# A new deal of expert slots and output tiles over the groups, and the values of a score chunk multiplied one group later than its scores

## The reference

```python
xn = _layernorm(x)
x = x + attention(xn, Wq, Wk, Wv, Wo, bo) + ffn(xn, gate_w, gate_b, w1, w2)
# attention: 16 heads of 64, rotary q and k, causal mask, softmax over 1024 keys, output matrix Wo
# ffn: each of 32 experts takes its 8 best tokens of a batch, weighted into one vector,
#      h = gelu([vec, 1] @ w1[e]); o = [h, 1] @ w2[e]; o is scattered back to the 8 tokens
```

## Time and profile before

| | us |
|---|---|
| median of 3 runs | 1545.79 (1543.32 to 1549.16) |
| the profiled execution, its time | 1545.64 |
| its span, first to last instruction | 1543.8 |
| PE busy in it | 1374.1 |
| POOL busy | 984.9 |
| DVE busy | 887.9 |
| ACT busy | 625.5 |

### The profile page before, as it was taken

One profiled execution on the slowest core, in us unless ns is written; L12 is line 12 of the kernel. 1 busy time (PEld: TensorE's weight loads), 2 busy tenths in 40 slices (PEclk: granted clock), 3 DMA queues, 4 the chain that ended last, 5 costly groups with the idle time before them and its releaser, 6 DMA issues.

```text
span 1543.8 us, 31034 instructions
## 1 busy us (share of the span) xinstructions
PE 1374.1 (89%) x11644; PEld 890.6 (58%) x11644; DVE 887.9 (58%) x1200; ACT 625.5 (41%) x919; POOL 984.9 (64%) x664
## 2 busy tenths in 40 slices
PE   3547889888988879999999999999999999999976
PEld 2334555454554546766666577666666776666646
DVE  7434555566464455567666655657666556656633
ACT  1213434334443433344444433544444435544431
POOL 1033655555554555688887865888887658888861
PEclk9778999898898999999999999999999999999999
DMA  5675665666556441212123322121232211222111
GB/s 202 255 241 189 237 203 198 213 213 214 198 200 226 159 139 56 82 65 70 57 83 111 94 70 67 59 90 57 70 101 94 93 59 61 81 72 70 43 46 55
DMA packets 112959, 188.85 MB, mean 122 GB/s; under 512 B 30064, under 2 KB 49936, under 8 KB 112432
## 3 DMA queue, kind: packets, MB, share of 16 engines
q1 hardware_dynamic: 85312, 115.39, 22.7%
q10 hardware_dynamic: 27456, 71.34, 13.6%
q0 software_dynamic: 48, 0.13, 0.0%
HBM read 130.58 MB, written 22.54 MB: 99 GB/s over the span
## 4 chain that ended last, share of the span: by engine, by line
PE 76%; DVE 6%; issue 5%; DMA 3%; ACT 3%; SPq 1%; POOL 1%; ACTq 0%; DVEq 0%; POOLq 0%
PE t_pO L1161 17%; PE t_pF L1136 13%; PE t_pA L1068 8%; PE t_pB L1068 6%; PE t_pF L1122 5%; PE t_pC L1210 3%; PE t_pB L1210 3%; PE t_pA L1092 3%; DVE t_OT L928 3%; PE t_pC L1170 2%; PE t_pC L1092 2%; PE t_pA L1073 2%; PE t_pB L1195 2%; PE t_pB L1073 2%; PE t_pB L1185 1%
## 5 line engine op out<-in xcount | busy, mean ns | idle before, releaser
L779 POOL TENSOR_TENSOR t_acc<-t_acc,t_PT 128x1024 f32<-128x1024 f32 (+3 forms) x256 | 444.4, 1736 | 203.4 <-ACT t_PT L814 183.7
L756 POOL TENSOR_TENSOR t_swap<-t_swap,s_sin 128x512 f32<-128x512 f32 x128 | 168.3, 1315 | 212.5 <-DMA t_swap<-t_raw 211.9
L1161 PE MATMUL t_pO<-t_PT,t_V 128*64 128x512 f32 (+3 forms) x1536 | 298.8, 511 | 4.4 <-ACT t_PT L814 4.4
L814 ACT ACTIVATE t_PT<-t_pA 128x1024 f32<-128x1024 f32 x192 | 169.6, 883 | 266.8 <-PE t_pA L1080 223.9
L1136 PE MATMUL t_pF<-t_xT,t_wqk 128*128 128x512 f32 x768 | 228.2, 435 | 17.2 <-DMA t_xT<-xt_s 12.0
L960 DVE TENSOR_TENSOR t_LO<-t_rot,t_HI 128x512 fp32r<-128x512 f32 x128 | 131.4, 1026 | 97.2 <-ACT t_HI L845 97.0
L759 POOL TENSOR_TENSOR t_rot<-t_rot,t_swap 128x512 f32<-128x512 f32 x128 | 180.7, 1412 | 10.0
L1161 PEld LDWEIGHTS t_pO<-t_PT,t_V 128*64 128x64 f32 x1536 | 95.8, 140 | 154.8 <-issue 133.5
L1136 PEld LDWEIGHTS t_pF<-t_xT,t_wqk 128*128 128x128 f32 x768 | 143.1, 200 | 62.8 <-issue 28.1
L936 DVE TENSOR_REDUCE s_nm<-t_pC 128x2 f32<-128x256 f32 (+2 forms) x96 | 72.0, 778 | 158.9 <-PE t_pC L1098 158.9
L835 ACT ACTIVATE t_raw<-t_pF 128x512 f32<-128x512 f32 x128 | 76.5, 598 | 199.3 <-PE t_pF L1136 181.7
(11 more groups left out here) (150 smaller groups left out, 2415.4 us busy)
## 6 DMA issues: line engine op xcount, KB each, us to landing
t_w1t<-in_L_ffn_w ACTq DMA_DIRECT2D x32, 1024.0 KB, 7.3
t_swap<-t_raw SPq DMA_DIRECT2D x256, 128.0 KB, 2.1
t_w2t<-in_L_ffn_w ACTq DMA_DIRECT2D x32, 1024.0 KB, 5.6
t_OT<-r_s SPq DMA_DIRECT2D x128, 128.0 KB, 2.9
t_wqk<-wqk_s SPq DMA_DIRECT2D x24, 512.0 KB, 4.2
xt_s<-a_xThl SPq DMA_DIRECT2D x16, 512.0 KB, 3.5
t_xT<-xt_s SPq DMA_DIRECT2D x8, 1024.0 KB, 6.3
t_wvs<-wv_s SPq DMA_DIRECT2D x12, 512.0 KB, 3.6
```

The costliest lines, as they stand in the source:

```text
L756: pool.tensor_tensor(swap[:, r % 2, :], swap[:, r % 2, :], sin[:, c * BANK:(c + 1) * BANK], ALU.mult).then_inc(sin_done, 1)
L779: pool.tensor_tensor(a[:, :, off:], a[:, :, off:], pt, ALU.add).then_inc(acc_done, 1)
L814: act.activation(PT[:, n % PTS, :, 0:w], bank[:, :, 0:w], ACT.Exp, scale=SCALE).then_inc(exp_done, 1)
L1161: mm = pe.matmul(pO[h * DH:(h + 1) * DH, off:], v, PT[:, n % PTS, h, 0:w], start=(j == 0), stop=(j == 4 * c + 3))
```

## The change

The slots of an expert group of four are dealt anew: group 0 has `layer1` of its own pair's fourth expert, group 1 none, group 2 a turn and a `layer2`, groups 3 to 5 a turn, a `layer1` and a `layer2` each. In a group PE now does the turn, the output tiles, the `layer1`, then the `values` of the **previous** group's chunks, then the `layer2`. DVE reads the turn right behind the maxima and the other slots at its end as before. ACT's gelu moves from the end of group 5 to the middle of group 1, and `copy_out` one group on. Output tiles of a batch start one group later and run singly except in group 1, over two pairs (for the last batch over the groups of P = 32).

```diff
 def slots_of(P, g):
     if P == -1:
-        return {2: [("layer1", 0, 0), ("layer1", 0, 1)], 3: [("layer1", 0, 2), ("layer1", 0, 3)]}.get(g, [])
-    if not 0 <= P < E // GE:
+        return {2: [("layer1", 0, 0), ("layer1", 0, 1)], 3: [("layer1", 0, 2)]}.get(g, [])
+    if not 0 <= P < E // GE or g == 1:
         return []
-    slots = [[("turn", P, 0), ("layer2", P, 0)], [("turn", P, 1), ("layer1", P + 1, 0)],
-             [("layer2", P, 1), ("layer1", P + 1, 1)], [("turn", P, 2), ("layer2", P, 2)],
-             [("turn", P, 3), ("layer1", P + 1, 2)], [("layer2", P, 3), ("layer1", P + 1, 3)]][g]
-    return [s for s in slots if s[0] != "layer1" or s[1] < E // GE]
+    if g == 0:
+        return [("layer1", P, 3)]
+    slots = [("turn", P, g - 2), ("layer1", P + 1, g - 3), ("layer2", P, g - 2)]
+    return [s for s in slots if s[0] != "layer1" or g > 2 and s[1] < E // GE]
 def outputs_of(P, g):
-    tiles = [(0, 1), (2,), (3,), (), (4, 5), (6, 7)][g]
-    return [(P // PAIRS - 1, t) for t in tiles] if P > 0 and P % PAIRS == 0 else []
+    y, p = divmod(P, PAIRS)
+    if P == N:
+        tiles = [(), (0, 1), (2,), (3,), (4, 5), (6, 7)][g]
+    else:
+        tiles = {0: [(), (0, 1), (2,), (3,), (4,), (5,)], 1: [(6,), (7,), (), (), (), ()]}.get(p, [()] * GROUPS)[g]
+    return [(y - 1, t) for t in tiles] if y > 0 else []
 # ACT
-                if normalise_of(P, g) is not None:
-                    copy_out(normalise_of(P, g))
                 if s and normalise_of(*STAGES[s - 1]) is not None:
+                    copy_out(normalise_of(*STAGES[s - 1]))
                     copy_sums(normalise_of(*STAGES[s - 1]))
...
+                if g == 1 and 0 <= P < E // GE:
+                    act.wait_ge(slot_read, SLOT["layer1", P, GE - 1] + 1)
+                    act.activation(gh[:, :, :], gh[:, :, :], ACT.Gelu).then_inc(g_done, 1)
                 f = fill_of(*STAGES[s - 2]) if s >= 2 else None
                 if f in ROPE:
                     high(f)
...
-                if ("layer1", P + 1, GE - 1) in slots_of(P, 3 if P == -1 else 5) and g == 5:
-                    act.wait_ge(slot_read, SLOT["layer1", P + 1, GE - 1] + 1)
-                    act.activation(gh[:, :, :], gh[:, :, :], ACT.Gelu).then_inc(g_done, 1)
 # DVE, behind the maxima
+                for x_ in slots_of(P, g):
+                    if x_[0] == "turn":
+                        read_slot(*x_)
...
                 for x_ in slots_of(P, g):
-                    read_slot(*x_)
+                    if x_[0] != "turn":
+                        read_slot(*x_)
 # PE
                 for x_ in slots:
-                    if x_[0] != "turn":
+                    if x_[0] == "layer1":
                         slot(*x_)
-                for c, j in chunks:
-                    values(P, c, j)
+                for c, j in chunks_of(*STAGES[s - 1]) if s else ():
+                    values(*pair_of(s - 1), c, j)
+                for x_ in slots:
+                    if x_[0] == "layer2":
+                        slot(*x_)
```

More of the change, by code:

```diff
@@ L604, in turns_before, with pair_of @@
             return sum((g == 1 and 0 <= P < N) + (g == 4 and 0 <= P + 1 < N) for P, g in STAGES[:s])
+        def pair_of(s):
+            return STAGES[s][:1]
         def nm_cols(a, n):
```

## The result

| | before | after |
|---|---|---|
| median | 1546.57 (1543.32 to 1549.16, 4 runs) | 1482.74 (1480.11 to 1487.24, 4 runs) |
| the profiled execution, its time | 1545.64 | 1482.14 |
| its span | 1543.8 | 1480.4 |

The ratio of after to before is 0.959, with a 95% interval of 0.956 to 0.962: 4.1% faster. The forecast was 1470, with a range of 1440 to 1508. The time is inside, 13 us above the forecast.

What follows compares the result with a forecast made beforehand. PE was taken to bound the kernel nearly everywhere, with removable time in slot pairs, output pairs and both ends. Gains of 39 (slots), 26 (outputs), 6 (start) and 5 (end) sum to 76: 1545.6 - 76 = 1470 us, range 1440 to 1508.

Steps and rivals of the forecast that it cites:

- the two old waits: Slot pairs, groups 0 and 3: layer2 waits for t_hT (42.7 us), group 0's exponential comes late (part of 34.5); both go.
- slots, pairs 1 to 7: Pairs 1 to 7: 78 us of stall and slow clock, less 39 of new waits with clock, gain 39 (bounds 5 and 78).
- outputs, pairs 8, 9, 16, 17, 24, 25: Output tiles: single round_outs and longer groups remove stalls; pairs 16 and 24 gain 8.8 - 0.5 each, pair 8 9.5; together 26.
- plain pairs: Pairs without slots or outputs: later values cost 0, with 7 us for the range; they stay at 34.67 us.
- `layer2` of group 3 behind the `layer1` read: Group 3, slot pairs: layer2 waits for DVE's layer1 read behind low and normalise, 1.6 us a pair (bounds 0 and 2.8).
- `t_D` behind the gelu: Before group 2's first scores: table load and gelu, 2.34 us, exceed slack 1.5; new wait 0.9 a pair (bounds 0 and 2).
- second scores behind the weights' remainder: Group 2's end: DVE makes the weights' remainder before reading layer2; wait 1.5 us in five of seven pairs (bounds 0 and 2.6).
- the 0.44 for an idle us: Pairs 1 to 7: each idle us of PE costs 0.44 us more through the slow clock behind it.
- 43.5: Length in us of a slot pair without stalls: 34.7 as in pair 10 plus 8.8 of slot work.
- rival B: layer1 read late in groups 3, 4 and 5, each waiting about 2.5 us: slots gain nothing, 1509 us; chance 0.13.
- The loads: w1 and w2 go out together in groups 4, 5 and 0, no transfer added: cost taken as 0, but close.
- rival D: Three groups in a row send 2 MB each, the queue backs up, w1 lands late: slower, 1601 us; chance 0.05.

Runs made afterwards that it cites:

- no_lag: Kernel after with the values multiplied in their own group again and copy_out back, both new deals kept: 1483.2 us, 0.960 of before.
- early_lag8: Kernel after with the layer1 read right behind the maxima, values one group later only in pairs 0 to 7, row sums stored first by SP: 1453.8 us.
- lag8_w2sp: The last run: kernel after with layer1 read behind the maxima, later values only in pairs 0 to 7, row sums first, w2 loads on SP behind swap: 1456.9 us.
- best: Kernel after with reciprocal and layer1 read behind the maxima, later values only in pairs 0 to 7, row sums stored first by SP: 1521.0 us.

## Why the prediction was right, and where its sizes were off

The mechanism held: the two old waits went, stalls came back in new places (51 of the 78 us, against 39 forecast), and the outputs gave what was forecast. Forecast and gain, from span to span (1543.8 to 1480.4):

| term | forecast | measured |
|---|---|---|
| slots, pairs 1 to 7 | 39 | 382.4 - 355.3 = 27.2 |
| outputs, pairs 8, 9, 16, 17, 24, 25 | 26 | 25.1 |
| start | 6 | 10.5 |
| end | 5 | 4.8 |
| plain pairs | 0 (7 named for the range) | -4.1 |
| sum | 76 | 63.4 |

Part of the nearness is luck: the start gave 4.5 us more than forecast, against 17 us less from all the other terms. Of the signs that were named, "plain pairs over 35" stood among those of being wrong, and 11 of the 17 were over it. Pairs 1 to 5 were to be near 50 and took 47.3 to 52.6; 6 and 7 were to be near 47.5 and took 59.4 and 43.0.

**Slots: the term that was mis-sized.** By its own parts, in us of idle time in pairs 1 to 7:

| wait of PE | forecast | measured |
|---|---|---|
| `layer2` of group 3 behind the `layer1` read | 11.2 | 8.4 |
| the same in group 5 | 2.1 | 6.3, of it 5.4 in pair 6 |
| `t_D` behind the gelu | 6.3 | 3.8 |
| second scores behind the weights' remainder | 7.5 | 1.1 |
| turn of group 2, behind `invert` | 0 | 9.9 |
| second scores of group 1, `layer1` read | 0 | 4.9 |
| an exponential | 0 | 4.2 |
| sum | 27 | 38.6 |

The waits that were forecast came out smaller, 19.6 us; 19.0 came from places that were costed at nothing. The 12 us for the slow clock came out as 12.0 by the same reckoning, so the whole miss of 12 us is idle time; but the 0.44 for an idle us is not confirmed, as a part of these 12.0 is found at full clock (pair 2, above).

Three steps of the sum do not hold. Pair 7 has no `layer1` for an eighth pair: its waits in groups 3 and 5, 1.9 us, were counted and can't arise, and it has about 3 us less work than 43.5 (PE busy 41.83 us, a clock of 0.98). The lower bound of the gain, 5, does not follow from the bounds of the waits, which give 7 x (2.8 + 2.8 + 2.0) + 5 x 2.6 = 66 us of idle time, more than there was. And rival B, three waits of 2.5 us in seven pairs, comes to "gain nothing" only if the waits for `t_D` and of the second scores are left out.

**The step that failed** is "The loads. [...] I take 0". It asked only whether PE would wait for `t_w1t` (it hardly does: 0.9 us, once; landing 4.8 to 10.4 us, median 6.5). What else shares the DMA engines was not asked. The swap, the row sums and the reciprocals are small transfers, each with an engine waiting, and some of them go out in the groups where 2 MB are now in flight. Without the `w2` loads 24 us more are gained. That is near rival D, but not its mechanism: not the weights come late, but small transfers behind them. Not all of the 19.0 us is theirs: without the `w2` loads 6.7 of it stay, most of it in pairs 1, 3 and 5, where the row sums stand behind the store of `wv_s`.

**The first wait, by row and rule.** In pair 3 the prediction kept the row's 2.83 us of `normalise` and made the wait 1.6; the rule of the Trainium skill, "SBUF — State Buffer", section "Who interferes with whom", gave 1.2. After, group 3 of pair 3 has:

```profile
300.09 4.89 POOL L786 TENSOR_TENSOR t_acc<-t_acc,t_PT 128x1024 f32<-128x1024 f32 x2 [0.49 <-ACT t_PT L821]
...
302.87 2.65 DVE L966 TENSOR_TENSOR t_LO<-t_rot,t_HI 128x512 fp32r<-128x512 f32 x1
305.45 0.68 DVE L934 TENSOR_TENSOR t_OT<-t_OT,t_OC 128x512 f32<-128x512 f32 x1
306.05 0.41 DVE L992 TENSOR_TENSOR t_g<-t_pB,t_b 128x256 f32<-128x256 f32 x1
...
306.51 1.07 PE L1205 MATMUL t_pC<-t_w2t,t_hT 128*32 128x256 f32 x16 [1.21 <-DVE t_g L992]
```

The instruction that is caught beside POOL is now `t_LO`, 2.65 us; `normalise` takes 0.68. The end of `t_LO`, 305.52, is POOL's end, 304.98, plus 0.54, the same offset as before. The duration belonged to POOL's end and not to `normalise`, and the wait came to 1.21. In this pair the rule gave the better number. It is not so everywhere: in pairs 1, 2, 4 and 5 `t_LO` begins just before POOL's second addition (201.98 and 202.31 in pair 1) and takes 0.74; `normalise` is caught again, for 2.84 us, and the wait is 1.50, nearer to the 1.6 of the row. In pair 6 it is as in pair 3. The six waits sum to 8.4 us, between 9.6 by the row and 7.2 by the rule.

**Plain pairs.** "PE has no idle time in pair 10 that would take up a delay, and 0.3 us a pair would cost 7 us" was right as a doubt. In pair 11 `t_LO` of group 0 took 2.27 us and PE stood 0.55 before the projection of group 1; in pair 10 it took 1.07 and PE did not stand:

```profile
664.77 2.27 DVE L966 TENSOR_TENSOR t_LO<-t_rot,t_HI 128x512 fp32r<-128x512 f32 x1
...
667.14 0.69 DVE L976 TENSOR_TENSOR t_rot<-t_pF,s_cos 128x512 f32<-128x512 f32 x1
...
667.94 1.62 PE L1146 MATMUL t_pF<-t_xT,t_wqk 128*128 128x512 f32 x6 [0.55 <-issue]
```

The row names no releaser; the projection overwrites `t_pF`, which DVE's `rope` had read by 667.83. The runs with the values in their own group from pair 8 on (`no_lag`, `early_lag8`, `lag8_w2sp`) have these pairs back at 34.7; `best`, with the late reciprocal as well, does not (36.0 in the mean).

**Outputs, start, end.** Pairs 8 and 9 took 98.9 (100 forecast), 16 and 17 took 97.0 (96). The output weights were 1.95 us late, not 3.0. The run with this part alone gained 24.7. At the start, the first scores began at 122.86 instead of 127.56 us, and pair 0 took 48.3 instead of 54.1. The forecast had summed the gelu, the turn and a `layer1` to 6; which of them gave the rest was not tried. At the end five waits ahead of tiles, 11.9 us with the one of 5.08, became four of 1.7 us, and the gain is 4.8.

## What to carry to other kernels

When large loads are moved, ask of every small transfer that goes out beside them who waits for its landing, and put round trips through HBM first in the issuing engine's list and ahead of the loads in time. An instruction that waits for such a round trip must not stand ahead of work for which the bounding engine waits; but moving it back is safe only if its own store does not then meet the next loads. A long duration next to another engine's work should be read as an end, not as a length.

## What the runs showed of the hardware

- A 128 KB transfer issued by SP lands in 3.3 us in the median with the 1 MB loads spread out, in 5.5 with two bunched, and in 12.6 at worst. That ACT issued the loads and SP the small ones did not keep them apart. The Trainium skill, "DMA: Bandwidth & Descriptors", section "Issuing engines are not separate DMA queues", says that transfers of all issuing engines run on the same 16 DMA engines and interleave there; the runs agree.
- Yet where a load stands in time counts. Issued by SP behind the swap, the same `w2` loads left the swap at a median of 3.1 us, and the store of the row sums behind them, in pair 1, took 8.9 until it could be read back. In both traces shown it was back within 0.3 us behind the 512 KB store that SP had issued just ahead of it (290.5 and 290.72; 194.2 and 194.38). Whether the one had to wait for the other, or both for the loads, was not tried.
- Shares of busy time did not show it: DMA is busy 0.59 of pairs 1 to 7 before and 0.65 after. In groups 0 and 1 of pair 3 it is 0.93 and 0.90.
- Why pair 6 stays long (14.2 us in group 2 and 12.6 in group 5 in the last run) is open. It has an extra 1 MB of `t_xT` in two of its groups; moving that load was not tried.
- In group 3 the VectorE instruction with two SBUF inputs that began behind the start of POOL's second addition ended 0.54 to 0.56 us behind its end, whichever it was: `normalise` in pair 3 before and in pair 1 after, `t_LO` in pair 3 after. It took 2.65 to 2.84 us; the other of the two took 0.68 to 0.74.
